# Three attentions of a fused transformer kernel rebuilt: fp32 scores in row groups, sums from a column of ones

## The reference

```
q, k, v = xn @ Wq.T + bq, ctx @ Wk.T + bk, ctx @ Wv.T + bv      # 16 heads of 8
s = (q @ k.T) / sqrt(8) + bias[256, 256]; masked keys to -inf   # per head and batch
x = x + tanh(g) * (softmax(s) @ v) @ Wo.T + bo                  # bo inside the gate
```

## Time and profile before

| | us |
|---|---|
| median of 3 runs (861.39 to 3578.52) | 862.42 |
| profiled execution, its own time | 862.37 |
| span from the first to the last instruction | 860.4 |
| busy PE / DVE / ACT / POOL | 702.3 / 573.1 / 488.9 / 166.6 |
| SP's transfers, MB | 31.36 |

### The profile page before, as it was taken

One profiled execution on the slowest core, in us unless ns is written; L12 is line 12 of the kernel. 1 busy time (PEld: TensorE's weight loads), 2 busy tenths in 40 slices (PEclk: granted clock), 3 DMA queues, 4 the chain that ended last, 5 costly groups with the idle time before them and its releaser, 6 DMA issues. The chain is left out here.

```text
span 860.4 us, 14382 instructions
## 1 busy us (share of the span) xinstructions
PE 702.3 (82%) x4728; PEld 396.0 (46%) x4728; DVE 573.1 (67%) x1765; ACT 488.9 (57%) x1323; POOL 166.6 (19%) x135
## 2 busy tenths in 40 slices
PE   4589994559997878999744899949999999869978
PEld 2266663336665323333222667635336666644322
DVE  3699995869996358667865999855316666436553
ACT  2288881259883568598812988812666556413201
POOL 8622000420000045536655000020000000000000
PEclk8689997769999768998885999979999999969999
DMA  8895004060000000000009200000000000000000
GB/s 310 169 319 177 2 7 69 23 126 2 2 2 2 0 1 0 1 0 1 1 0 180 41 2 2 2 26 0 1 0 1 1 2 2 1 1 1 0 1 24
DMA packets 22056, 32.26 MB, mean 38 GB/s; under 512 B 1760, under 2 KB 15712, under 8 KB 21216
## 3 DMA queue, kind: packets, MB, share of 16 engines
q1 hardware_dynamic: 21984, 31.36, 14.4%
HBM read 21.39 MB, written 9.96 MB: 36 GB/s over the span
## 5 line engine op out<-in xcount | busy, mean ns | idle before, releaser
L816 ACT ACTIVATE RING<-RING,NMX 128x256 f32<-128x256 f32 x384 | 190.7, 500 | 56.2 <-DVE NMX L1637 55.8
L1637 DVE CUSTOM_DVE_ANT_0 RING<-bank,ADJM 128x256 f32<-128x256 f32 x384 | 143.4, 413 | 23.5 <-DMA scratch<-RING 22.5
L1158 PE MATMUL bank<-W,RING 128*128 128x128 f32 x768 | 120.5, 282 | 15.6 <-ACT RING L828 13.9
L541 POOL TENSOR_TENSOR small<-small 128x8 f32<-128x8 f32 (+2 forms) x13 | 17.7, 1365 | 463.1 <-DVE small L1528 463.1
L1158 PEld LDWEIGHTS bank<-W,RING 128*128 128x128 f32 x768 | 91.7, 145 | 27.9 <-ACT RING L816 23.2
L1138 PE MATMUL bank<-ARENA 128*128 128x256 bf16 x384 | 77.8, 290 | 30.7 <-DMA ARENA<-scratch 25.7
L1649 DVE COPY RING<-bank 128x512 f32<-128x512 f32 x144 | 98.6, 686 | 1.2 <-PE bank L1158 0.8
L816 ACT ACTIVATION_READ_ACCUMULATOR RING<-RING,NMX 128x1 f32 x384 | 72.8, 190 | 0.0
L997 PE MATMUL bank<-XT,W 128*128 128x512 f32 (+2 forms) x118 | 62.2, 668 | 6.6 <-ACT XT L712 5.3
L728 ACT ACTIVATE RING<-bank,NMX 128x512 f32<-128x512 f32 x64 | 43.4, 683 | 41.8 <-PE bank L1062 21.2
L1280 PE MATMUL bank<-ARENA,W 64*128 64x512 f32 x180 | 62.3, 710 | 3.6 <-DVE ARENA L1830 2.3
(11 more groups left out here) (253 smaller groups left out, 1307.3 us busy)
## 6 DMA issues: line engine op xcount, KB each, us to landing
scratch<-ARENA SPq DMA_DIRECT2D x18, 256.0 KB, 3.2
ARENA<-scratch SPq DMA_DIRECT2D x6, 768.0 KB, 10.6
W<-in_weights SPq DMA_DIRECT2D x1, 2564.0 KB, 21.2
scratch<-RING SPq DMA_DIRECT2D x36, 64.0 KB, 3.0
ARENA<-scratch SPq DMA_DIRECT2D x12, 192.0 KB, 3.8
scratch<-RING SPq DMA_DIRECT2D x18, 128.0 KB, 2.9
ARENA<-scratch SPq DMA_DIRECT2D x6, 384.0 KB, 6.6
W<-in_weights SPq DMA_DIRECT2D x2, 1024.0 KB, 13.7
```

The costliest lines, as they stand in the source:

```text
L816: nc.scalar.activation(P_OF(n)[:, q * S:(q + 1) * S], S_OF(n)[:, q, :], ACT.Exp, bias=NMX[:, 2 * t + q:2 * t + q + 1], scale=-1.0, accum_o ...
L1158: mm = nc.tensor.transpose(bk[:, o:o + P], P_OF(n)[:, i:i + P], ident)
L1637: nc.vector.tensor_tensor_reduce(out=S_OF(n)[:, q, :], in0=SBANK(n)[:, q * S:(q + 1) * S], in1=ADJM[:, b, q, :], scale=-1.0, scalar=BIG, o ...
```

## The change

The attentions 0, 1 and 2 are rebuilt; nothing of the scratch tensors is left.

- Keys and queries are projected straight into place: PE makes 32 output rows per head at row 32j (`heads`, four heads in four column groups, 16 products a piece), and QT and KT hold head j of group g in rows 32j to 32j+7, in fp32. The bias columns are spread the same way by 16 small products (`biases`).
- A step m is four heads and 128 queries, thus two units t = 2m, 2m+1. Its four score products have 8 rows each, in four row groups, and write four banks. These have no second copy: `Scores.fill` has PE wait until all four are emptied.
- Only the first 256 queries and half of the keys are made ahead of the loop. The rest (`extra`: values, keys, queries) and the output bias row are made inside it, between two score steps, in the score banks: five places in attentions 0 and 2, two in attention 1, whose keys and values are made in the stage before. ACT and DVE share the evacuation.
- V has a column of ones after each head's 8 (a pitch of 9), so the value product gives the sums as a ninth row. ACT no longer sums. PE turns the output of a group back to tokens (ONE_T), DVE takes reciprocals and multiplies; once per batch PE turns it again (BACK_T) and makes one product of 128 rows with output weights that 16 small transfers pack (`compact`).
- DVE and ACT copy every second unit's transposes each (before: three of four and one of four).
- Loads are reordered (context ahead of the weights). In attention 0 DVE makes the masks of batch 0 first and those of the others at t = 6 inside the loop; POOL makes the masks of two batches of attentions 1 and 2 in the stage before, and clears only V.

```diff
-LAG, PV_T, OTR_T, SEL_T, OUT_T = 3, 8, 9, 13, 27
-PT_SLOTS = 7
+LAG, PV_T, OTR_T, ONE_T, BACK_T, OUT_T, END_T = 3, 8, 9, 13, 27, 31, 16
...
+PITCH = DH + 1
+EXTRAS = [[("q", 0), ("v", 0), ("q", 1), ("k", 2), ("q", 2)], [("q", 0), ("q", 1), ("q", 2)],
+          [("q", 0), ("v", 0), ("q", 1), ("k", 2), ("q", 2)]]
...
+        QT = ARENA[:, 0:4096].rearrange("p (g t) -> p g t", g=4)
+        KT = ARENA[:, 4096:8192].rearrange("p (g t) -> p g t", g=4)
+        PT = ARENA[:, 8192:12288].rearrange("p (s j k q) -> p s j k q", s=2, j=4, k=2)
         V = ARENA[:, 14336:14336 + NT * VW].rearrange("p (t f) -> p t f", t=NT)
-        KF, QF = ARENA[:, 15616:16640], ARENA[:, 16640:17664]
...
+        OTR = ARENA[:, 15680:16192].rearrange("p (s q) -> p s q", s=2)
+        ON = ARENA[:, 16192:16704].rearrange("p (s q f) -> p s q f", s=2, q=2)
+        OTN2 = ARENA[:, 16704:17216].rearrange("p (s q) -> p s q", s=2)
+        WOC = [ARENA[:, 20224:20352], ARENA[:, 20352:20480], w("wk0")]
...
+            def compact(a):
+
+                at = COL[f"wo{a}"][0]
+                for g in range(NG):
+                    for j in range(HG):
+                        sp.dma_start(WOC[a][PAD * g + DH * j:PAD * g + DH * (j + 1), :],
+                                     w_in[PAD * j:PAD * j + DH, at + g * P:at + (g + 1) * P]).then_inc(s_wo[a], 16)
+
...
-            write_keys(0)
-            sp.wait_ge(s_zero, 1)
-            read_keys(0)
-            queries(0)
...
+            def clear_values():
+
+                nc.gpsimd.memset(ARENA[:, 14336:14336 + NT * VW], 1.0).then_inc(s_zero, 1)
...
-                                                 accum_out=SUMS[:, 2 * t + q:2 * t + q + 1]
+                        if n >= 6:
+                            act.wait_ge(s_t, n - 5)
+                        for i in range(2):
+
+                            nc.scalar.activation(P_OF(n)[:, i * S:(i + 1) * S], S_OF(n)[:, i, :], ACT.Exp,
+                                                 bias=NMX[:, 2 * t + i:2 * t + i + 1], scale=-1.0
                                                  ).then_inc(s_exp, 1)
...
-                            act.wait_ge(s_fa, PV_AT[a] + (u - PT_SLOTS) // 4 + 1)
-                        nc.scalar.activation(PT_OF(n), TBANK(n)[:, :], ACT.Copy).then_inc(s_te, 1)
+                        if GG >= 2:
+
+                            act.wait_ge(s_pv, GG - 1)
+                        nc.scalar.activation(PT[:, GG % 2, 2 * jj:2 * jj + 2, :, q * P:(q + 1) * P],
+                                             TBANK(n)[:, :].rearrange("p (i k q) -> p i k q", i=2, k=2),
+                                             ACT.Copy).then_inc(s_te, 1)
...
+            def heads(out, name, g, rhs):
+
+                for j in range(HG):
+                    f = DH * (HG * g + j)
+                    mm = nc.tensor.matmul(out[PAD * j:PAD * j + PAD, :], w(name, f, f + PAD), rhs, start=True,
+                                          stop=True)
+                return mm
...
+            def extra(a, kind, k, scores):
+
+                x, (t0, t1) = extra_no(a, kind, k), PIECES[k]
+                scores.fill(pe, [(s_xa, 2 * x + 2), (s_xd, 2 * x + 2)])
+                for g in range(NG):
+                    if kind == "q":
+                        mm = heads(bank[g][:, 0:t1 - t0], f"wq{a}", g, XT[:, t0:t1])
+                    elif kind == "k":
+                        mm = heads(bank[g][:, 0:t1 - t0], f"wk{a}", g, CT[:, t0:t1])
+                    else:
+                        mm = value_tiles(a, bank[g], 2 * g, 2 * g + 2)
+                    mm.then_inc(s_xf, 1)
...
+                for t in range(UNITS + END_T):
+                    if t < UNITS and t % 2 == 0:
+                        m = t // 2
+                        b, g, q = m // 8, m // 2 % 4, m % 2
+                        if a != 1 and m == 1:
+                            extra(a, "v", 0, scores)
+                        if a != 1 and m == 3:
+                            out_row(a, ra, s_fa)
+                        if a != 1 and m == 8:
+                            extra(a, "k", 2, scores)
+                        if m in (4, 12):
+                            extra(a, "q", m // 8 + 1, scores)
...
+                        for j in range(HG):
+
+                            r = slice(PAD * j, PAD * j + DH)
+                            mm = nc.tensor.matmul(bank[j][:, 0:S], QT[r, g, b * S + q * P:b * S + (q + 1) * P],
+                                                  KT[r, g, b * S:(b + 1) * S], start=True, stop=True)
+                            if j % 2 == 1:
+                                mm.then_inc(s_s, 1)
                     u = t - LAG
...
+                        if n >= 2:
+
+                            pe.wait_ge(s_te if n % 2 else s_to, n // 2)
...
+                            pe.wait_ge(s_te, 2 * GG + 2)
+                            pe.wait_ge(s_to, 2 * GG + 2)
+                            pe.wait_ge(s_otr, GG)
...
+                            f = PITCH * (HG * g + j)
+                            mm = nc.tensor.matmul(bank[6][PAD * j:PAD * j + PAD, 0:S], V[:, 2 * b + part, f:f + PAD],
+                                                  PT[:, GG % 2, j, part, :], start=(part == 0), stop=(part == 1))
...
+                    if t >= ONE_T and (t - ONE_T) % 4 == 0 and (t - ONE_T) // 4 < UNITS // 4:
+
+                        G = (t - ONE_T) // 4
+                        GG, b = base // 4 + G, B * a + G // 4
...
+                        if G % 4 == 1:
+                            pe.wait_ge(s_res, TPB * b)
+                        for q in range(TPB):
+                            mm = nc.tensor.transpose(bank[7][:, q * P:(q + 1) * P],
+                                                     OTR[:, GG % 2, q * P:(q + 1) * P], ident)
...
+                        for q in range(TPB):
+                            mm = nc.tensor.transpose(bank[7][:, q * P:(q + 1) * P], ON[:, i % 2, q, :], ident)
+                        mm.then_inc(s_back2, 1)
...
+                            o = bank[7][:, q * P:(q + 1) * P]
+                            nc.tensor.matmul(o, OTN2[:, i % 2, q * P:(q + 1) * P], WOC[a], start=True, stop=False)
...
+            def first_masks():
+
+                dve.wait_ge(s_ldm, 32)
+                mask_terms(0, 1)
+                for q in range(TPB):
+                    nc.vector.scalar_tensor_tensor(ADJM[:, 0, q, :], ADJM[:, 0, q, :], NANQ[:, q:q + 1],
+                                                   ADJ[:, 0, q, :], ALU.add, ALU.add).then_inc(s_adjm, 1)
...
+            def other_masks():
+
+                dve.wait_ge(s_ldm2, 48)
+                mask_terms(1, B)
+                link(nc.vector.tensor_reduce(NANB, PADM[:, :, :], AX.X, ALU.min))
                 link(nc.vector.tensor_scalar(NANB, NANB, BIG, 1e9, ALU.mult, ALU.mult))
...
+                        if a == 0 and t == 6:
+                            other_masks()
+                        if a != 1 and t == 16:
+                            extra(a, "k", 2)
+                        if t in (8, 24):
+                            extra(a, "q", t // 16 + 1)
                         dve.wait_ge(s_adjm, (a * B + b + 1) * TPB)
-                        if n >= 3:
-                            dve.wait_ge(s_exp, 2 * n - 4)
+                        if n >= 4:
...
+                        src = bank[7][:, 0:S].rearrange("p (q j r) -> p q j r", q=2, j=HG)
+                        link(nc.vector.reciprocal(RS, src[:, :, :, DH:PITCH]))
+                        nc.vector.tensor_tensor(
+                            ON[:, i % 2, :, PAD * g:PAD * g + PAD].rearrange("p q (j d) -> p q j d", j=HG),
+                            src[:, :, :, 0:DH], RS.to_broadcast([P, TPB, HG, DH]), ALU.mult).then_inc(s_on, 1)
...
```

More of the change, by code:

```diff
@@ L30 @@
 PW = NG * P
-VW = H16 * DH + PAD - DH
+VW = 168
 NE = 8
@@ L515, in _ @@
-            read_keys(2)
-            queries(2)
+            compact(2)
             sp.wait_ge(s_var, 9)
```

539 lines of the change are left out of this document (240 added, 299 removed).

## The result

| | before | after |
|---|---|---|
| median of 4 runs, us | 862.59 (861.39 to 862.76, and one of 3578.52) | 882.9 (879.35 to 883.45) |
| span of the profiled execution, us | 860.4 | 881.3 |
| mean granted clock of PE | 0.898 | 0.919 |

The ratio is 1.0232, 95% interval 1.0196 to 1.0267; the run of 3578.52 us is not part of it. The forecast was 853, in a range of 814 to 895: the time lies in the range, on the other side of the kernel before. Between the profiled spans the program grew by 20.9 us where the sum had -9.2; 30 us are to be found.

A forecast was written before the change was run, and what follows sets the result against it. DVE was taken to fill the loops' groups of 4.98 us, with PE nearly always busy. Starts -55.2, loops +10.0, half clock +2, projections and masks +41.5, tails -7.5 sum to -9.2: 853 us, range 814 to 895.

The forecast's parts named there:

- The starts: Time to each attention's first row maximum: -23.9, -12.2 and -21.1 us, against +2 for DVE slower beside POOL.
- The step in the loop: A group of four units as two steps takes 5.57 us for 4.98; +3.1, +3.3 and +3.6 for the loops.
- the short step: Loop step without value products: scores wait until all four banks are emptied; 2.27 us, 18 of 32 steps.
- A change of tiling: PE switching between full and column tiling: 0.09 us, plus 0.05 for weights that can't be loaded ahead.
- The long step: Loop step with the value products, set by PE's own work: 3.3 us, 14 of 32 steps.
- The output products: Three output products inside each loop, adding 0.7 us each (1.35 of PE, 0.65 of it hidden).
- my third rival: Loop: transposes wait for ACT's late copy, so the hand-over stretches the long step too; 888 us, chance 0.19.
- The tails: From last maximum to last residual in each attention: 7.5 us for 10.0, three times, -7.5 in all.
- The clock early in the loops: PE at half clock only in attention 1's first steps: +2 us.
- The projections of 512 columns: Keys or queries inside the loop add their whole length: 4.5 us; queries of 256 columns 2.5, values 2.4.
- The bias row and the other masks: Inside the loop: bias row 1.2 us; in attention 0 the other masks on DVE 4.3.
- The second case: Rival: DVE and ACT set the loop's pace, 4.9 us per group, projections 12 less; about 818 us, chance 0.24.

The follow-up runs named there:

- masks3: balance with values, second queries and bias row computed beside the scores, and DVE's masks of the first attention in three pieces: 857.16 us (0.9969).
- pairs: Changed kernel; in every second score step heads 0 and 1 wait for their own two banks only: 884.32 us (1.0268).
- bf16sc: Changed kernel with queries and keys in bf16, one pass per score product, less exact: 852.93 us (0.9903).
- balance: Changed kernel with the second half of the value products moved from long to short step, a group's output copy one unit later: 859.53 us (0.9952).
- tail2: balance with last transposes ahead of the last-but-one group's second values, its turn ahead of the last values, five unused small products: 856.13 us (0.9956).
- tail3: tail2 without the five small products: 857.22 us (0.9950).
- together: Changed kernel with both halves of the value products behind the second set of transposes, two tiling changes fewer per group: 871.4 us (1.0123).
- warm: Changed kernel with an additional unused product (256 columns) in each of the first six steps of each loop: 881.37 us (1.0232).

## Why the prediction was wrong

**The starts** were right in sum. Predicted -23.9, measured -22.9; from the end of attention 0 to the next first maximum 42.77 became 32.99, -9.8 for the sum of -12.2 and +2. That agreement is luck: up to the layer norm the stage took 20.56 for 20.63, so the 2 us for DVE beside POOL did not come, and from the norm to the first maximum 22.14 became 12.43, -9.7 for -12.2; the 16 head products took 3.64 us there at the lower clock and 1.93 ahead of attention 2. From the third layer norm to the first maximum 30.98 became 9.47: -21.5 for -21.1. POOL clears for 1.22 us instead of 6.93 and more:

```profile
455.39 1.22 POOL L545 MEMSET ARENA<- 128x1344 f32 x1 [11.18 <-DVE ARENA L1940]
```

**The routed stage between attentions 1 and 2** was to stay. It took 159.4 us for 165.1, and 159.2 to 162.2 in 14 of the 15 other profiles (166.7 in that of masks3). Part of it is the clock, in these rows of before and after (the same stage, 21 us apart); the rest is open:

```profile
380.00:400.00 20.00, 18.52 (x54) 6.19 (x54) 15.47 (x22) 15.85 (x24) 11.39 (x10) 0.89 0.00 0
```

```profile
400.00:420.00 20.00, 19.50 (x62) 6.54 (x58) 15.52 (x25) 18.82 (x28) 12.93 (x10) 1.00 0.01 1
```

**The step in the loop is the first that failed**, by its hand-overs. I had 2.27 for the short step: 0.71 to the result, 1.47 of maxima, two hand-overs of 0.05. The result was right, each hand-over is three times that: 0.15 from DVE to the scores and 0.16 from the scores to DVE (the profile models the end of a product, so the split between result and second hand-over is less sure than their sum, 0.87). A change of tiling was priced right (0.14). The long step came to 3.39 for 3.3; the score step next to a wait takes 0.73, not 0.64. 18 x 0.22 and 14 x 0.09 are 5.2 us per loop. The output products gave 1.3 of it back: the sum had three of them at 0.7, and there are two ahead of the last maximum, at 0.38 each. So the steps account for 3.9 us per loop, 12 in all. pairs shows that the short step is this chain, bf16sc that 0.41 of it is the second pass, balance that it had 0.57 us of room that the program did not use. Of my third rival only the name fits, a hand-over that makes steps longer. The wait that it described (ACT's copy late) was not there: L801's releases cost PE 2.1 us in the whole program, all of it in the tails.

```profile
L1168 PE MATMUL bank<-ARENA 8*128 8x256 f32 x768 | 73.9, 448 | 32.6 <-DVE NMX L1693 22.4
L1200 PE MATMUL bank<-ARENA 128*32 128x256 f32 x768 | 62.0, 398 | 2.1 <-ACT ARENA L801 2.1
```

**The tails failed** by 13 us, the largest part: predicted 7.5 each from the last maximum's end, measured 12.27, 11.09 and 12.18. In the first one the terms that were too small are: exponentials 1.54 for 0.95, since ACT does a copy and earlier exponentials first; transposes 2.5 for 0.7, since they stand behind values and a turn in PE's program order; the turn 1.0 for 0.45, since bank 7 is still held by the group before; the output product 2.97 for 1.1, of which 0.65 is that the product with its bias takes 1.77 at full clock and 1.2 is the lower clock. tail2 and tail3 show that the order matters little: in tail3 the last set of transposes no longer stands behind the second values, and PE then waits 0.50 for ACT's copy out of the single bank 6. The fault was to add the durations of one chain as if each engine stood ready.

**The clock early in the loops** is the third. The projections of 512 columns cost 4.5 exactly as forecast (7.01 less 2.49); in attentions 0 and 1 those of 256 columns cost 4.8 and 4.4 for 2.5, in attention 0 the values 4.8 for 2.4, because PE ran at 1.2 GHz (in attention 2, where the queries met the full clock, they cost 2.5):

```profile
39.77 3.64 PE L1011 MATMUL bank<-XT,W 128*32 128x256 f32 x32 [2.78 <-DVE NMX L1693]
...
58.97 3.64 PE L1011 MATMUL bank<-CT,W 128*32 128x512 f32 x32 [0.67 <-DVE NMX L1693]
```

The first row is 256 columns, the second 512, in the same time. Beyond the steps at full clock the loops are 10 us over the sum, 7 in the first, 1 in the second, where I had +2 for it, and 2.6 in the third; most of it is these early steps. The bias row and the other masks, 1.0 us under their forecast together in the first loop, are counted in. The forecast took its clock from the earlier trace rows, a stretch in which PE hardly idles; here the first steps leave it idle for a quarter to a third of the time. The Trainium skill (TensorE: Matmul & The Clock Gate, Part 4: PE-mode transpose) says that transposes do not count as busy for the clock; the early steps would fit that, the settled loop, with as many transposes at full clock, does not, so no run here decides it.

Together: loops +22 over the forecast (12 from the steps, 10 mostly from the clock), tails +13, the stage between -6, starts +1: the 30.

**Chances.** 0.24 was given to slower, most of it to the third rival at 888. The time came out at 883, near that rival but by other steps, so it lies in the stated range by luck. The second case's 818 does not follow from its own terms: 853 - 30 - 12 is 811, under the range's lower end of 814. The forecast took its hand-overs at 0.05 from rows where DVE was never the one waiting; there was no row of before for a small tiling behind a wait, and the term should have been bounded from above by 0.16 as the result's delay was.

## What to carry to other kernels

When the banks between two engines exist once, the loop's step is a closed chain (product, result, reading, release), and each hand-over in it is paid in full: write that chain down with hand-overs bounded from both sides, then look whether the engine's idle time in the short step could take work of the long one, which was worth 23 us here for one changed condition and one constant. Multiply a price per step by a count taken from the list of steps. Price a tail as a list of who holds which bank and what stands ahead in each program, not as a sum of durations.

## What the runs showed of the hardware

- A change between full and column tiling cost 0.14 us with the next weights (0.28 for two, together). Four products of 8 rows by 256 columns, two passes each, took 0.71 in four row groups; with one pass 0.29.
- From the last score pass to a waiting maximum 0.16 passed, in fp32 and in bf16 (0.17), from transposes to a waiting copy 0.03 (88.16 to 88.19). The ends of products are modelled in the profile, and no run tells why the two differ.
- Over ten runs of one program the mean granted clock goes from 0.909 to 0.927 and the time from 866.75 to 850.28 (balance). Unused products in PE's early waits raised it (0.926 to 0.932 for 0.919 to 0.924) and left the time of the changed kernel as it was (warm, 881.37 for 882.9).
